# Moving one product and two pieces of one bank's traffic in a selective scan with a routed feed-forward, on one core

## The chip, the cores and the metric

The kernel runs on one core of a Trainium2 chip, in one launch. The metric is the time on the device in microseconds. TensorE is called PE, VectorE DVE, ScalarE ACT, GpSimd POOL and SyncE SP, as in the profile.

## The reference, cut to what matters

Eight sequences of 512 tokens with 256 channels go through a Mamba-like layer and then through a mixture of eight experts. Only the first layer is touched. With 512 inner channels and 16 states for each:

```
h   = silu(conv4(norm(x) @ in_proj_w.T))                  # (512 inner channels) x (512 tokens)
proj = h @ x_proj_w.T                                     # 1 + 16 + 16 rows: dt_in, B, C
dt  = softplus(dt_in @ dt_proj_w.T + dt_proj_b)
state_t = exp(A * dt_t) * state_(t-1) + B_t * h_t         # for each of 512 channels x 16 states
y_t = sum_n state_t[n] * C_t[n] + D * h_t
out = silu(y) @ out_proj_w.T + shortcut
```

All arithmetic is float32. The experts come after all eight sequences.

## The kernel before, in words

Each iteration scans one sequence `i`. Channels lie on the partitions, tokens on the free axis. A step `q` of 32 handles one state `n` (16) for one half of the channels (2), as tiles of 128 x 1024: two groups of 128 channels by 512 tokens. A step consists of:

- `decays` (ACT, L742): exp(A dt) into one of two rings in the bank `psX`, two instructions. It needs the scan two steps back.
- `inject`: the product B x into a ring of four `bx` tiles. For even `q` POOL makes it (L502), from a copy `bbc` of B's row that a DMA has spread over the partitions. For odd `q` DVE makes it (L1080), from the bank `psB`, into which PE has spread B's row with a matmul (`spread_b`, L1454) that waits for DVE's product before.
- `scan` (DVE, L1092): the recurrence along the tokens, into a ring of eight `state` tiles.
- `weigh` (POOL, L513): times C's row, in place. It waits for the scan. POOL's order in an even step is `inject(q + 4)`, then `weigh(q)`.
- `total` (PE, L1497): adds the tile up in `psY`, three steps later; the tile is then free for the scan eight steps on.

Beside this, iteration `i` carries the front of sequence `i + 1` (`front`: projection, convolution, softplus) and the back of sequence `i - 1` (`back`: output projection, norms), cut up by step numbers. Front and back share one bank, `psF`, in turn. Each engine executes its own list in the written order; semaphores connect them. What matters here:

- Step 12 and 13: ACT reads z from `psF` (L644) for the softplus. Step 14: PE multiplies the rows dt_in, B and C into `psF` (L1387, `w_bc`); ACT takes |z| (L650) and then copies the rows out into `prow` (L652).
- Steps 15 and 17: PE makes the two halves of the output projection in `psF` (L1419), the first once `prow` is copied, the second once DVE has read the first. Steps 16 and 18: DVE adds them to `ao` (L1050).
- POOL subtracts for the softplus after `weigh(20)` (`loss`, L518). ACT squares after it (L667), and DVE takes the smaller of the two in steps 23 and 24 (L1041), each after that step's scan.

Iterations 0, 1, 6 and 7 are written out; 2 to 5 run in a loop of two iterations on DVE, ACT and POOL. There the counts that semaphores are compared with are computed in registers.

Of the kernel before, what the change touches and what calls it, by code (L numbers as in the profile page):

```python
# [19 lines left out]
def build(nc, x, winT, conv_w, xprojT, dt_w, dt_b, A_log, D, woutT, norm_w, norm_b,  # L20
# [15 lines left out]
    H = 2  # L36
    CH = C // H
    Q = H * N
    PN = N // 2
    PQ = H * PN  # L40
    DQ = Q - PQ
    RD = 2
    RB = 4
    RS = 8
# [16 lines left out]
    with ctx:  # L61
# [264 lines left out]
        def _(sp):  # L326
# [30 lines left out]
            def load_b(f, par, g):  # L357
                if g == 0:
                    sp.wait_ge(rows_stored, 16 * (f + 1))
                if not (isinstance(f, int) and f == 0):  # L360
                    sp.wait_ge(pool_bx, PQ * (f - 1) + PN + CG * (g + 1))
                src = rows(f)[:, 0:N].rearrange("a (m two) t -> a two m t", two=2)[:, 0, CG * g:CG * (g + 1)]
                sp.dma_start(bbc[:, CG * g:CG * (g + 1)], src.broadcast_to([P, CG, L])).then_inc(b_loaded[g], 16)

# [119 lines left out]
        def _(pool):  # L484
# [34 lines left out]

            def iteration(i, par, do_front):  # L520
                for q in range(Q):
                    if q % 2 == 0:
                        if q + RB < Q:
                            inject(i, par, q + RB)
                        elif do_front:
                            inject(i + 1, 1 - par, q + RB - Q)
                    weigh(i, q)
                    if do_front and q == 20:
                        loss(i + 1, 1 - par)
# [57 lines left out]
        def _(act):  # L587
# [37 lines left out]
            def front(f, par, q):  # L625
# [14 lines left out]
                if q in (12, 13):  # L640
# [5 lines left out]
                    if q == 13:  # L646
                        last.then_inc(z_done, 1)
                if q == 14:
                    act.wait_ge(z_done, f + 1)
                    nc.scalar.activation(tmp[:], acc[:], ACT.Abs).then_inc(sf, 1)  # L650
                    act.wait_ge(proj_ready, f + 1)
                    nc.scalar.activation(prow[par][:], psF[:], ACT.Identity).then_inc(prow_kept, 1)  # L652
                if q == 15:
                    act.wait_ge(sf, 2 * f + 1)
                    nc.scalar.activation(tmp[:], tmp[:], ACT.Exp, scale=-1.0).then_inc(u_ready, 1)
# [329 lines left out]
        def _(dve):  # L985
# [90 lines left out]

            def inject(i, par, q):
                h, n = divmod(q, N)
                dve.wait_ge(b_bcast, i * DQ + q // 2 + 1)
                nc.vector.tensor_tensor(bx[q % RB][:], xh[par][:, h * CH:(h + 1) * CH],  # L1080
                                        psB[:].unsqueeze(1).broadcast_to([P, CH, L]), ALU.mult).then_inc(dve_bx, 1)

            def scan(i, q):
                k = i * Q + q
                if q % 2 == 0:
                    dve.wait_ge(pool_bx, i * PQ + q // 2 + 1)
                else:
                    dve.wait_ge(dve_bx, i * DQ + q // 2 + 1)
                dve.wait_ge(decay_ready, k + 1)
                if not (isinstance(k, int) and k < RS):  # L1090
                    dve.wait_ge(summed, k - RS + 1)
                nc.vector.tensor_tensor_scan(st[q % RS][:].rearrange("p c t -> p (c t)"),  # L1092
                                             decay[q % RD].rearrange("p c t -> p (c t)"),
                                             bx[q % RB][:].rearrange("p c t -> p (c t)"),
                                             0.0, ALU.mult, ALU.add).then_inc(scanned, 1)

            def iteration(i, par, do_lead, do_front, do_scan, do_back, do_choose=True):
                for q in range(Q):
                    if do_scan:
                        scan(i, q)  # L1100
                        if q % 2 == 0:
                            inject(i, par, q + 1)
                    if do_scan and not do_front and q in (12, 13, 14, 15):
                        early_act(q - 12)
                    if do_back:
                        back(i - 1, q)
                    if do_choose and q == 20:
                        choose(i - 2)
                    if do_front:
                        front(i + 1, 1 - par, q)  # L1110
                    if do_lead:
                        lead(i + 2, par, q)
# [194 lines left out]
        def _(pe):  # L1307
# [140 lines left out]
            def spread_b(i, par, q):  # L1448
# [1 line left out]
                if q == 1:  # L1450
                    pe.wait_ge(prow_kept, i + 1)
                if not (isinstance(i, int) and i == 0 and q == 1):
                    pe.wait_ge(dve_bx, i * DQ + q // 2)
                nc.tensor.matmul(psB[:], ident[:, n:n + 1].broadcast_to([P, P]), prow[par][:],  # L1454
                                 start=True, stop=True).then_inc(b_bcast, 1)

# [52 lines left out]

            def iteration(i, par, do_front, do_scan, do_back):  # L1510
                for q in range(Q):
                    if q % 2 == 1:
                        if q + 2 < Q:
                            if do_scan:
                                spread_b(i, par, q + 2)
                        elif do_front:
                            spread_b(i + 1, 1 - par, q + 2 - Q)
                    if do_scan and q >= SUM_LAG:
                        total(i, par, q - SUM_LAG)
                    elif do_back:  # L1520
                        total(i - 1, 1 - par, q + Q - SUM_LAG)
                    if do_front:
                        front(i + 1, 1 - par, q)
                    else:
                        early(q)
                    if do_back:
                        back(i - 1, q, do_front)
                    if q == 19 and i >= 2:
                        choose(i - 2)
# [170 lines left out]
```

## Time and profile before

| | us |
|---|---|
| three timed runs, median (lowest, highest) | 1506.67 (1503.97, 1511.75) |
| the profiled execution, its own time | 1497.41 |
| its span, first to last instruction | 1495.6 |
| mean granted TensorE clock, share of full | 0.904 |

The scans take up the first 1006 us of the span, the experts the rest. In the table of busy time an engine's idle time counts only where something later waits for it. The profiled execution was shorter than each of the three timed runs, so sums are made against its own time.

### The profile page before, as it was taken

Reading aid. Unit: us, or ns where it says so; the run is one execution under the profiler, and the core shown is the slowest. Engines: PE = TensorE matmul, PEld = TensorE weight load, DVE = VectorE, ACT = ScalarE, POOL = GpSimd, SP = SyncE. Lnnn points to the kernel's source line nnn. Section 1 sums busy time; section 2 is a strip of 40 time slices with the busy share of each in tenths; the row PEclk is TensorE's granted clock in tenths of the full one; section 3 lists DMA queues with packets and bytes.
Section 4 is the critical chain, followed back from the end, with each engine's and each line's share of the span. In section 5 each row is a group of like instructions: output and inputs, shape, how many; then the busy total and the mean of one; then the engine's idle time right before and its main releaser. Section 6 shows DMA issues by size and latency. Waiting matters only on the chain.

```text
span 1495.6 us, 15504 instructions
## 1 busy us (share of the span) xinstructions
PE 1187.9 (79%) x4766; PEld 523.0 (35%) x4767; DVE 1020.1 (68%) x1059; ACT 802.4 (54%) x1387; POOL 1016.0 (68%) x476
## 2 busy tenths in 40 slices
PE   4775868879878787797887877974999999999940
PEld 2221223224223222331332322423455656666620
DVE  4697998898998989899899897871311123322237
ACT  6666568658668677677766865554111111111137
POOL 0599999999999999999999999990363000000035
PEclk9897899999899899899889988996999999999975
DMA  3801301220230240240150131021954011111135
GB/s 103 320 0 58 119 23 58 98 85 31 89 123 2 99 142 2 76 164 1 58 169 1 59 127 56 1 71 56 370 202 151 0 39 42 44 47 42 39 116 179
DMA packets 78243, 129.54 MB, mean 87 GB/s; under 512 B 7648, under 2 KB 56416, under 8 KB 74080
## 3 DMA queue, kind: packets, MB, share of 16 engines
q1 hardware_dynamic: 68624, 112.07, 22.1%
q0 software_dynamic: 3072, 8.39, 1.7%
q10 hardware_dynamic: 6480, 8.26, 1.6%
q8 instruction: 32, 0.52, 0.1%
q14 instruction: 35, 0.29, 0.1%
HBM read 96.46 MB, written 32.24 MB: 86 GB/s over the span
## 4 chain that ended last, share of the span: by engine, by line
PE 35%; POOL 33%; issue 13%; DVE 11%; ACT 7%; DMA 1%; POOLq 0%; DVEq 0%; ACTq 0%
POOL state L513 19%; POOL bx L502 10%; PE psX L1606 10%; PE psX L1555 6%; DVE state L1092 5%; PE bank L1623 2%; PE psY L1623 2%; PE psY L1497 2%; POOL fy L579 2%; PE psY L1576 2%; PE bank L1576 2%; PE bank L1419 2%; DVE acc L1027 2%; POOL lt L518 1%; PE bank L1454 1%
## 5 line engine op out<-in xcount | busy, mean ns | idle before, releaser
L513 POOL TENSOR_TENSOR state<-state,cbc 128x1024 f32<-128x1024 f32 x256 | 606.2, 2390 | 11.2 <-DVE state L1092 11.0
L1092 DVE TENSOR_TENSOR_SCAN state<-psX,bx 128x1024 f32<-128x1024 f32 x256 | 577.5, 2278 | 38.0 <-ACT psX L742 23.9
L742 ACT ACTIVATE psX<-dt,aneg 128x511 f32<-128x511 f32 x512 | 330.5, 678 | 205.4 <-DVE state L1092 203.7
L502 POOL TENSOR_TENSOR bx<-xh,bbc 128x1024 f32<-128x1024 f32 x128 | 309.5, 2418 | 58.8 <-DMA bbc<-bc_rows 42.0
L1497 PE MATMUL psY<-state,ident 64*64 64x512 f32 x2048 | 293.9, 664 | 27.1 <-POOL state L513 26.8
L1454 PE MATMUL bank<-prow,ident 128*128 128x512 f32 x256 | 166.5, 737 | 114.1 <-DVE bx L1080 113.9
L579 POOL DMA_INDIRECT fy<-slot_out,slot x32 | 33.2, 1037 | 316.6 <-DMA slot_out<-yo 307.1
L1080 DVE TENSOR_TENSOR bx<-xh,bank 128x1024 f32<-128x1024 f32 x128 | 152.9, 1195 | 7.9 <-PE bank L1454 7.8
L1497 PEld LDWEIGHTS psY<-state,ident 64*64 64x64 f32 x2048 | 63.5, 142 | 218.2 <-issue 134.4
L1244 DVE TENSOR_TENSOR actN<-sg,psX 128x512 f32<-128x512 f32 x39 | 26.8, 687 | 141.3 <-ACT sg L930 141.3
L1454 PEld LDWEIGHTS bank<-prow,ident 128*128 128x128 f32 x256 | 47.3, 219 | 204.5 <-DVE bx L1080 168.0
L930 ACT ACTIVATE sg<-psX 128x512 f32<-128x512 f32 x39 | 23.3, 597 | 155.5 <-PE psX L1606 155.5
L1201 DVE TENSOR_TENSOR actS<-sg,psX 128x512 f32<-128x512 f32 x28 | 19.2, 687 | 106.5 <-ACT sg L904 106.5
L1606 PE MATMUL psX<-wg,xsT 128*128 x156 | 77.2, 617 | 1.2 <-DVE xsT L1238 0.6
L1606 PE MATMUL psX<-wu,xsT 128*128 x156 | 73.3, 592 | 0.0
L1374 PE MATMUL bank<-lt,win 128*128 128x512 f32 x112 | 55.5, 618 | 19.4 <-DVE acc L1027 18.0
L1419 PE MATMUL bank<-wout,yv 128*128 128x256 f32 x256 | 61.5, 395 | 8.9 <-ACT yv L688 7.9
L1027 DVE SCALAR_TENSOR_TENSOR acc<-bank,cw,acc 128x511 f32<-128x511 f32 (+2 forms) x84 | 62.3, 741 | 3.3 <-ACT acc L633 1.2
L904 ACT ACTIVATE sg<-psX 128x512 f32<-128x512 f32 x28 | 16.7, 597 | 81.3 <-PE psX L1555 81.3
L1419 PEld LDWEIGHTS bank<-wout,yv 128*128 128x128 f32 x256 | 48.8, 195 | 28.6 <-issue 12.7
L1555 PE MATMUL psX<-xg,shg 128*128 128x512 f32 x112 | 54.6, 611 | 1.7 <-DVE actS L1201 1.7
L1555 PE MATMUL psX<-xg,shu 128*128 128x512 f32 x112 | 52.8, 593 | 0.0
(193 smaller groups left out, 1547.3 us busy)
## 6 DMA issues: line engine op xcount, KB each, us to landing
cbc<-bc_rows SPq DMA_DIRECT2D x32, 1024.0 KB, 5.0
bbc<-bc_rows SPq DMA_DIRECT2D x16, 1024.0 KB, 6.2
slot_in<-ao SPq DMA_DIRECT2D x1, 4992.0 KB, 27.4
xsl<-slot_in SPq DMA_DIRECT2D x39, 128.0 KB, 2.2
slot_out<-yo ACTq DMA_DIRECT2D x39, 128.0 KB, 2.4
xin<-in_x SPq DMA_DIRECT2D x8, 512.0 KB, 4.4
xr<-in_x SPq DMA_DIRECT2D x8, 512.0 KB, 5.4
x_rows<-ao SPq DMA_DIRECT2D x8, 512.0 KB, 2.9
```

The source lines that it names most:

```text
L502: nc.gpsimd.tensor_tensor(bx[q % RB][:], xh[par][:, h * CH:(h + 1) * CH], bbc[:, n // 2].unsqueeze(1).broadcast_to([P, CH, L]), ALU.mult). ...
L513: nc.gpsimd.tensor_tensor(w[:], w[:], cbc[:, n].unsqueeze(1).broadcast_to([P, CH, L]), ALU.mult).then_inc(weighted, 1)
L579: nc.gpsimd.indirect_dma_start(out=fy[q % FRING][:, t % 2, :], out_offset=None, in_=y_d, in_offset=bass.IndirectOffsetOnAxis(slot[:, t:t + ...
L742: e = nc.scalar.activation(decay[q % RD][:, c, 1:L], dt[par][:, h * CH + c, 1:L], ACT.Exp, scale=aneg[:, h * CH + c, n:n + 1])
L1027: last = nc.vector.scalar_tensor_tensor(out=acc[:, c, m:L], in0=psF[:, 0:L - m], scalar=cw[:, c, TAPS - 1 - m:TAPS - m], in1=acc[:, c, m:L ...
L1080: nc.vector.tensor_tensor(bx[q % RB][:], xh[par][:, h * CH:(h + 1) * CH], psB[:].unsqueeze(1).broadcast_to([P, CH, L]), ALU.mult).then_inc ...
L1092: nc.vector.tensor_tensor_scan(st[q % RS][:].rearrange("p c t -> p (c t)"), decay[q % RD].rearrange("p c t -> p (c t)"), bx[q % RB][:].rea ...
L1419: last = nc.tensor.matmul(psF[:, (j % 2) * DIM:(j % 2 + 1) * DIM], yv[:, c, j * P:(j + 1) * P], wout[:, c], start=(c == 0), stop=(c == C - 1))
L1454: nc.tensor.matmul(psB[:], ident[:, n:n + 1].broadcast_to([P, P]), prow[par][:], start=True, stop=True).then_inc(b_bcast, 1)
L1497: done = nc.tensor.matmul(psY[o * HP:(o + 1) * HP, r], weights(half, c), src[half, c], start=first, stop=last_)
L1555: last = nc.tensor.matmul(bank, w[:, k, c * P:(c + 1) * P], xg[i][:, k], start=(k == 0), stop=(k == KC - 1))
L1606: last = nc.tensor.matmul(bank, xsT[i][:, k], w[:, bass.ds(ereg[i], 1), k].rearrange("p a n -> p (a n)"), start=(k == 0), stop=(k == KC - 1))
```

## The change

Four edits:

1. In ACT's step 14 the copy of the rows out of `psF` comes before |z|.
2. In PE's steps 15 and 17 the output projection comes before the sum (`total`) of that step, and no longer behind it.
3. The product B x of step 22 passes from POOL to DVE. DVE makes 17 of 32 products of an iteration, POOL 15.
4. All counts that go by these products follow: 15 and 17 for each iteration where 16 and 16 stood. SP's load of the next B rows (group 0) now waits for the eleventh product of POOL, that of step 20, where it waited for that of step 22.

```diff
+    BY_POOL = [q % 2 == 0 and q not in (22,) for q in range(Q)]
+    PQ = sum(BY_POOL)
     DQ = Q - PQ
+    NTH_P = [sum(BY_POOL[:q]) for q in range(Q + 1)]
+    NTH_D = [q - sum(BY_POOL[:q]) for q in range(Q + 1)]
...
-                    sp.wait_ge(pool_bx, PQ * (f - 1) + PN + CG * (g + 1))
+                    sp.wait_ge(pool_bx, PQ * (f - 1) + NTH_P[N + 2 * CG * (g + 1)])
...
-                    if q % 2 == 0:
+                    if BY_POOL[(q + RB) % Q]:
                         if q + RB < Q:
                             inject(i, par, q + RB)
...
                 if q == 14:
+                    act.wait_ge(proj_ready, f + 1)
+                    nc.scalar.activation(prow[par][:], psF[:], ACT.Identity).then_inc(prow_kept, 1)
                     act.wait_ge(z_done, f + 1)
                     nc.scalar.activation(tmp[:], acc[:], ACT.Abs).then_inc(sf, 1)
-                    act.wait_ge(proj_ready, f + 1)
-                    nc.scalar.activation(prow[par][:], psF[:], ACT.Identity).then_inc(prow_kept, 1)
...
-                dve.wait_ge(b_bcast, i * DQ + q // 2 + 1)
+                dve.wait_ge(b_bcast, i * DQ + NTH_D[q] + 1)
...
-                        if q % 2 == 0:
+                        if q + 1 < Q and not BY_POOL[q + 1]:
                             inject(i, par, q + 1)
...
-                    if q % 2 == 1:
+                    if not BY_POOL[(q + 2) % Q]:
                         if q + 2 < Q:
                             if do_scan:
                                 spread_b(i, par, q + 2)
...
+                    if do_back and q in (15, 17):
+                        back(i - 1, q, do_front)
                     if do_scan and q >= SUM_LAG:
                         total(i, par, q - SUM_LAG)
...
-                    if do_back:
+                    if do_back and q not in (15, 17):
                         back(i - 1, q, do_front)
```

PE's order around steps 14 to 18 of iteration 1 before (`xh,w_bc` is the projection of the rows, `prow,ident` the spreading of B, `wout,yv` the output projection, `state,ident` the sums, eight matmuls each, of which a row shows four where the two halves print apart):

```order
L1387 MATMUL bank<-xh,w_bc 128x512 x4
L1454 MATMUL bank<-prow,ident 128x512
L1497 MATMUL psY<-state,ident 64x512 x4
L1419 MATMUL bank<-wout,yv 128x256 x8
L1497 MATMUL psY<-state,ident 64x512 x4
L1454 MATMUL bank<-prow,ident 128x512
L1497 MATMUL psY<-state,ident 64x512 x4
L1419 MATMUL bank<-wout,yv 128x256 x8
L1497 MATMUL psY<-state,ident 64x512 x4
```

The same place now, with the line numbers of the changed file:

```order
L1390 MATMUL bank<-xh,w_bc 128x512 x4
L1457 MATMUL bank<-prow,ident 128x512
L1422 MATMUL bank<-wout,yv 128x256 x8
L1500 MATMUL psY<-state,ident 64x512 x8
L1457 MATMUL bank<-prow,ident 128x512
L1422 MATMUL bank<-wout,yv 128x256 x8
L1500 MATMUL psY<-state,ident 64x512 x8
```

One sum stood between the spreading and the first half of the projection, and none does now; the second half has also moved up by one sum.

DVE's order in steps 19 to 23 of iteration 1 before, from the scans of steps 19 and 20 on (`xh,bank` is the product B x, `psX,bx` the scan, `bank,xr` the sum for x1, `lt,dt` the minimum of step 23):

```order
L1092 SCALAR_TENSOR_TENSOR state<-psX,bx 128x1024 x2
L1080 TENSOR_TENSOR bx<-xh,bank 128x1024
L1092 SCALAR_TENSOR_TENSOR state<-psX,bx 128x1024 x2
L1080 TENSOR_TENSOR bx<-xh,bank 128x1024
L1060 TENSOR_TENSOR ao<-bank,xr 128x512
L1092 SCALAR_TENSOR_TENSOR state<-psX,bx 128x1024
L1041 SCALAR_TENSOR_TENSOR lt<-lt,dt 128x1024
```

And now:

```order
L1095 SCALAR_TENSOR_TENSOR state<-psX,bx 128x1024 x2
L1083 TENSOR_TENSOR bx<-xh,bank 128x1024
L1095 SCALAR_TENSOR_TENSOR state<-psX,bx 128x1024
L1083 TENSOR_TENSOR bx<-xh,bank 128x1024
L1095 SCALAR_TENSOR_TENSOR state<-psX,bx 128x1024
L1083 TENSOR_TENSOR bx<-xh,bank 128x1024
L1063 TENSOR_TENSOR ao<-bank,xr 128x512
L1095 SCALAR_TENSOR_TENSOR state<-psX,bx 128x1024
L1044 SCALAR_TENSOR_TENSOR lt<-lt,dt 128x1024
```

The product of step 22 now stands between the scans of steps 21 and 22, ahead of the minimum. On POOL the product of step 22 stood ahead of `weigh(18)`, and nothing took its place.

## Rows read from the trace of the kernel before

**Rows 1.** The page: the chain that ended last, by engine and by line
```profile
PE 35%; POOL 33%; issue 13%; DVE 11%; ACT 7%; DMA 1%; POOLq 0%; DVEq 0%; ACTq 0%
POOL state L513 19%; POOL bx L502 10%; PE psX L1606 10%; PE psX L1555 6%; DVE state L1092 5%; PE bank L1623 2%; PE psY L1623 2%; PE psY L1497 2%; POOL fy L579 2%; PE psY L1576 2%; PE bank L1576 2%; PE bank L1419 2%; DVE acc L1027 2%; POOL lt L518 1%; PE bank L1454 1%
```
**Rows 2.** Windows from loss to loss: stretch, length, busy us (instructions) of each engine
```profile
135.99:259.98 123.99, 91.18 (x390) 31.35 (x394) 109.32 (x80) 77.83 (x122) 116.78 (x50) 0.86 0.18 60
...
618.53:737.45 118.92, 96.82 (x416) 34.22 (x420) 108.61 (x95) 85.64 (x142) 117.51 (x51) 0.90 0.22 76
737.45:856.38 118.93, 96.00 (x432) 34.25 (x428) 107.18 (x86) 85.66 (x142) 117.61 (x51) 0.92 0.22 72
```
**Rows 3.** Waits in 618.5 to 737.4: total us, times, longest
```profile
DVE ao L1050 <- PE bank L1419: 3.6, 2, 3.1
...
POOL state L513 <- DVE state L1092: 1.4, 1, 1.4
```
**Rows 4.** Timeline of POOL, iteration 4: start, length, xcount [idle before]
```profile
611.59 2.37 POOL L513 TENSOR_TENSOR state<-state,cbc 128x1024 f32<-128x1024 f32 x1 [1.59 <-DVE state L1092]
613.92 2.35 POOL L502 TENSOR_TENSOR bx<-xh,bbc 128x1024 f32<-128x1024 f32 x1
...
618.53 4.53 POOL L518 TENSOR_TENSOR lt<-lt,dt 128x2048 f32<-128x2048 f32 x1
...
625.32 3.35 POOL L502 TENSOR_TENSOR bx<-xh,bbc 128x1024 f32<-128x1024 f32 x1
```
**Rows 5.** Timeline of DVE, iteration 4
```profile
590.00 1.19 DVE L1080 TENSOR_TENSOR bx<-xh,bank 128x1024 f32<-128x1024 f32 x1
591.38 4.47 DVE L1092 TENSOR_TENSOR_SCAN state<-psX,bx 128x1024 f32<-128x1024 f32 x2 [0.19 <-DVE bx L1080]
...
600.04 0.69 DVE L1050 TENSOR_TENSOR ao<-bank,ao 128x512 f32<-128x512 f32 x1 [3.07 <-PE bank L1419]
...
606.78 0.69 DVE L1050 TENSOR_TENSOR ao<-bank,ao 128x512 f32<-128x512 f32 x1 [0.56 <-PE bank L1419]
...
609.25 4.44 DVE L1092 TENSOR_TENSOR_SCAN state<-psX,bx 128x1024 f32<-128x1024 f32 x2
...
614.99 4.47 DVE L1092 TENSOR_TENSOR_SCAN state<-psX,bx 128x1024 f32<-128x1024 f32 x2
...
...
625.11 1.34 DVE L1041 SCALAR_TENSOR_TENSOR lt<-lt,dt 128x1024 f32<-128x1024 f32 x1 [1.75 <-ACT dt L667]
```
**Rows 6.** Timeline of PE, iteration 4
```profile
594.31 1.02 PE L1454 MATMUL bank<-prow,ident 128*128 128x512 f32 x2
595.26 1.09 PE L1497 MATMUL psY<-state,ident 64*64 64x512 f32 x8
596.28 3.72 PE L1419 MATMUL bank<-wout,yv 128*128 128x256 f32 x16
```
**Rows 7.** Timeline of ACT, iteration 4
```profile
594.51 0.60 ACT L652 ACTIVATE prow<-bank 128x512 f32<-128x512 f32 x1 [0.77 <-PE bank L1387]
...
598.03 1.28 ACT L742 ACTIVATE psX<-dt,aneg 128x511 f32<-128x511 f32 x2
...
623.09 1.91 ACT L667 ACTIVATE dt<-tmp 128x2048 f32<-128x2048 f32 x1 [2.17 <-POOL lt L518]
```
**Rows 8.** Timeline of POOL, then of DVE, iteration 0
```profile
101.23 2.35 POOL L513 TENSOR_TENSOR state<-state,cbc 128x1024 f32<-128x1024 f32 x1 [0.35 <-DVE state L1092]
...
142.50 8.25 DVE L1041 SCALAR_TENSOR_TENSOR lt<-lt,dt 128x1024 f32<-128x1024 f32 x1 [6.87 <-ACT dt L667]
```
**Rows 9.** Timeline of POOL, then of DVE, iteration 7
```profile
964.51 4.66 POOL L513 TENSOR_TENSOR state<-state,cbc 128x1024 f32<-128x1024 f32 x2
992.22 13.91 POOL L513 TENSOR_TENSOR state<-state,cbc 128x1024 f32<-128x1024 f32 x6
...
963.02 4.43 DVE L1092 TENSOR_TENSOR_SCAN state<-psX,bx 128x1024 f32<-128x1024 f32 x2
...
999.34 2.29 DVE L1092 TENSOR_TENSOR_SCAN state<-psX,bx 128x1024 f32<-128x1024 f32 x1
```

More of the change, by code:

```diff
@@ L39, in build @@
     PN = N // 2
-    PQ = H * PN
+    BY_POOL = [q % 2 == 0 and q not in (22,) for q in range(Q)]
+    PQ = sum(BY_POOL)
     DQ = Q - PQ
+    NTH_P = [sum(BY_POOL[:q]) for q in range(Q + 1)]
+    NTH_D = [q - sum(BY_POOL[:q]) for q in range(Q + 1)]
     RD = 2
@@ L1084, in scan @@
                 k = i * Q + q
-                if q % 2 == 0:
-                    dve.wait_ge(pool_bx, i * PQ + q // 2 + 1)
+                if BY_POOL[q]:
+                    dve.wait_ge(pool_bx, i * PQ + NTH_P[q] + 1)
                 else:
-                    dve.wait_ge(dve_bx, i * DQ + q // 2 + 1)
+                    dve.wait_ge(dve_bx, i * DQ + NTH_D[q] + 1)
                 dve.wait_ge(decay_ready, k + 1)
@@ L1100, in iteration @@
                         scan(i, q)
-                        if q % 2 == 0:
+                        if q + 1 < Q and not BY_POOL[q + 1]:
                             inject(i, par, q + 1)
@@ L1452, in spread_b @@
                 if not (isinstance(i, int) and i == 0 and q == 1):
-                    pe.wait_ge(dve_bx, i * DQ + q // 2)
+                    pe.wait_ge(dve_bx, i * DQ + NTH_D[q])
                 nc.tensor.matmul(psB[:], ident[:, n:n + 1].broadcast_to([P, P]), prow[par][:],
```

## The prediction, written before the changed kernel ran

> **What bounds the kernel now.** I read the chain of waits first [rows 1]. It points at POOL: its two operations of a step, L513 and L502, hold 29% of the chain, and the chain's PE part belongs mostly to the experts, which the change doesn't touch. A reader could stop here and say: every product taken from POOL is worth its duration. So the second view is one that can contradict this, the windows from one `loss` to the next [rows 2]. Such a period is 118.9 us long. POOL is busy for 117.5 us of it, DVE for 108.6 us. POOL is nearly full, but not full.
>
> The third view, the waits in the same stretch, says who holds the remaining 1.4 us: POOL waits once for a scan [rows 3]. The timelines say where. In iteration 4 `weigh(19)` starts at 611.59 after an idle 1.59 us [rows 4]; scan 19 had ended about 611.5 (the two scans 19 and 20 start at 609.25 and take 2.2 each [rows 5]). So once in each period POOL, for all its load, is released by DVE. A period is therefore a closed loop through several engines, and I follow it round:
>
> - `weigh(19)` at 611.59, product 24, `weigh(20)`, `loss` from 618.53 to 623.06 on POOL [rows 4];
> - the square on ACT, 623.09 to 625.00 [rows 7], which DVE had awaited for 1.75 us;
> - the minimum of step 23 on DVE at 625.11 [rows 5]. From there DVE works through steps 24 to 31 and 0 to 19 of the next sequence and ends scan 19 one period later.
>
> The first two legs take 625.11 - 611.59 = 13.5 us, the DVE leg 118.9 - 13.5 = 105.4 us. POOL's own loop is 118.9 - 1.4 = 117.5 us. The mixed loop is the longer, by 1.4 us, and sets the period.
>
> In the DVE leg DVE has one long wait, 3.07 us before its add at 600.04 for the first half of the output projection, and 0.56 us before the second at 606.78 [rows 5]; together 3.6 us in each period [rows 3].
>
> **Edit 1, the rows ahead of |z|.** The row that decides is the copy of the rows at 594.51: ACT had been idle for 0.77 us before it, waiting for PE [rows 7]. |z| was already over. So the copy can't come earlier by this edit: 0 us. |z|, 1.8 us, now falls behind the copy and pushes ACT's later pieces back. The first to feel it are the decays of step 18, at 598.03 now [rows 7]; with |z| ahead of them they start 1.8 us later and end at 601.1. Scan 18 follows scan 17, which starts 0.6 us after the first add, so at 599.6 with the gain of edit 2, and scan 18 at 601.8. They are 0.7 us in time. By step 19 ACT waits for DVE again, so the shift is gone. From both sides: nothing gained, since ACT waited anyway; lost at most the 1.8 us of |z| if these decays missed their scan. I take 0.
>
> **Edit 2, the projection ahead of the sums.** PE makes the spreading of B at 594.31, the sum of step 12 at 595.26 and the projection at 596.28 [rows 6]. The copy of the rows ends at 595.11 [rows 7]. With the sum behind it the projection starts at about 595.26: 596.28 - 595.26 = 1.02 us earlier. It takes as long as before, and DVE's add starts at 599.02. DVE still waits 2.05 us there. The second half starts after the first, two sums and one spreading; the distance between the halves had two sums and one spreading too, so it shifts by the same 1.02 us and isn't gained twice. Scan 19 ends 1.02 us earlier. The sums 12 and 14 come 3.7 us later, but the scans that need their tiles are those of steps 20 and 22, ten and more us away. Bounds: 0, if the first half had to wait for the copy, which leaves only 0.15 us; 3.6 us, if all of DVE's wait went. I take 1.0, since the matmuls stand without a gap between the rows.
>
> **Edit 3, the product of step 22.** POOL loses one product, 613.92 to the next start about 2.31 us later [rows 4]. It stood before `weigh(18)`, ahead of the place where POOL waits for scan 19. In a period that the mixed loop sets, this 2.31 us is only added to POOL's idle time: 1.4 + 2.3 - 1.0 = 2.7 us. It is worth 0 there.
> DVE gains the product: 1.19 us, and 0.19 us until the scan that depends on it starts, together 1.38 us (590.00 to 591.38, [rows 5]). It stands between scans 21 and 22. That is in the stretch in which DVE waits for the square: the minimum starts at 625.11 after 1.75 us of idling behind scan 23 [rows 5], which is over at 623.36. 1.75 - 1.38 = 0.37 us of cover remain, so the cost is 0. If the cover were gone, the minimum would move. PE must spread the row between product 21 and 22: product 21 is over at 614.8 and spreading takes 1.0, while DVE is at scan 21 until 617.2. Ready in time. PE waits there with sums 17 to 19 behind it, by at most 4 us; their tiles are needed at scans 25 to 27.
>
> How thin the cover is shows in the contention. DVE's minimum reads two SBUF tiles. It asks at 625.11, while POOL works; POOL's next product, at 625.32, is 3.35 us long where others are 2.35 [rows 4]: the minimum went first and POOL stood still for 1 us. In iteration 0 it went the other way: the same instruction took 8.25 us [rows 8], three POOL instructions long. The Trainium skill (SBUF — State Buffer, the section on the two separate sides) says that the pair of ports shared by the two is an exclusive lock, held for a whole instruction; by that, who comes late waits for a whole instruction of the other. The two rows agree with it in kind. It would leave the sum as it is while the minimum asks before 625.3.
>
> **Edit 4, the counts.** In the loop of iterations 2 to 5 DVE computes one more register value ahead of each product. Ahead of a product stands a scan of 2.2 us, under which the queue can work ahead: in the loop two scans in a row, with register instructions between them, take 4.44 us from start to end [rows 5], two bare durations. So 0. The upper bound is the gap that a register instruction leaves where the wait is exposed, 0.19 us [rows 5], on 13 products of the DVE leg and 4 iterations: 10 us. SP's earlier load of B rows has nobody who waits for it: 0.
>
> **The sum.** Iteration 0 has no back, and POOL runs from 101.23 on without a gap [rows 8] up to `loss`. There the product counts in full: -2.3. Iterations 1 to 6 close six mixed loops: 6 x -1.02 = -6.1. From `weigh(19)` of iteration 6 on POOL has no `loss` to share and idles no more; iteration 7's product counts, unless DVE is late. `weigh(19)` came at 964.51 + 2.31 = 966.8 and scan 19 ended at 965.2; both shift, to 964.5 and 964.3. At the end scan 31 was over at 1001.6 [rows 9], and would be at 1001.6 - 1.0 + 1.2 = 1001.8; `weigh(31)`, the last of six from 992.22, began at 1003.8 and could now begin at 1001.5. It waits 0.3: -2.0. Sum -2.3 - 6.1 - 2.0 = -10.4 us.
>
> The profiled execution took 1497.41 us, so the same execution would take 1487.0, or 0.7% less. The timed runs have their median at 1506.67, 9.3 us above the profiled one. By the same share the median is 1506.67 x 0.9931 = 1496 us, which I forecast.
>
> **Rivals.**
> A. POOL sets the period after all, because DVE's wait for the projection goes altogether (for instance ACT's and PE's work before it starts earlier too). Then each of eight iterations gives the whole product, 8 x 2.31 = 18.5 us: 1488. For it: POOL's 29% of the chain and 117.5 of 118.9 us. Against it: 2.05 us of the wait hang on the z, row and projection steps, which are not touched. 12%.
> B. Iteration 0's minimum wins against POOL this time. The loop from `loss` of iteration 0 to that of 1 would lose what it now has over the others, 124.0 - 118.9 = 5.1 us [rows 2]: 1506.67 - 15.5 = 1491. The alignment there doesn't change. 10%.
> C. The cover of 0.37 us isn't enough: the minimum asks after POOL's next instruction has begun and waits for one more, 2.3 us, in each of six periods: -10.4 + 13.9 = +3.5, 1510. It decides once scan 23 ends 0.2 us later than POOL's boundary allows, so with 0.6 us more than I reckon (ACT's later |z|, x1's sum that comes behind the product, or exposed register work). 12%.
> D. The change loses: the minimum of step 23 loses the lock to POOL, as in iteration 0, in the periods too. One such loss is 5.1 us; six are 30.6: -10.4 + 30.6 = +20, 1527. It decides from three losses on, where the gain is used up. For it: one in seven did so, and its request came at the same distance from POOL's boundary, 0.2 us, as those that won, so something that I can't see decides. Against it: six of seven won. 5%.
> E. The projection doesn't move, because the copy of the rows comes later than PE is free: only the ends gain, 4.3 us: 1502. 11%.
>
> The forecast has 50%. Less than 0.5%, 7.5 us, can't be told from no change. Faster: forecast, most of it, A and B, 66%. The same: E, C's better part, and the forecast's weak tail, 24%. Slower: D and C with exposed registers, 10%. The range leaves out D and the far end of A: 1484 to 1510; the low end is A with most of B's 5.1 us, the high end is C. The forecast's own range is 1491 to 1501.
>
> **What would show it.** The windows from loss to loss: 117.9 us, with POOL busy 115 and idle 2.7. The wait before DVE's first add: 2.05 us, where it was 3.07, and the second still 0.56. The projection's start follows the spreading without a sum between. ACT's idle before the row copy: about 2.6, where it was 0.77, and the copy no earlier. The wait for the square before the minimum: 0.4 where it was 1.75. Wrong I am if the first wait is unchanged (E), if POOL's idle stays near 1.4 at a period of 116.6 (A), if the minimum's wait is gone and the minimum lasts over 2 us (C) or over 6 us (D).

## The result, and the profile after

The changed kernel takes 1493.5 us (median of 4 runs, 1491.3 to 1493.7), the kernel before 1506.8 (4 runs beside them, 1504.0 to 1511.8). The ratio is 0.9905, with a 95% interval of 0.9877 to 0.9932: 13.3 us faster between the medians. The forecast was 1496, within 1484 to 1510. Here and below, single executions that took far longer than the rest (1526.6 us in experiment 1, 2697 in 2, 2028 in 3, 2022 in 6) are left out of the ratios and their intervals, not of the medians.

The windows from loss to loss in the trace of the changed kernel answer to [rows 2]: the stretch, its length, busy us and instructions of PE, PEld, DVE, ACT and POOL, TensorE's granted clock, the share of DMA and GB/s.

```profile
136.66:258.79 122.13, 91.97 (x402) 31.89 (x402) 115.06 (x85) 78.86 (x124) 114.43 (x49) 0.90 0.18 61
...
612.06:728.81 116.75, 96.29 (x427) 33.95 (x427) 109.74 (x95) 85.65 (x142) 115.30 (x49) 0.92 0.23 78
728.81:846.90 118.09, 94.39 (x427) 34.70 (x428) 108.43 (x87) 85.51 (x142) 115.23 (x49) 0.94 0.22 72
```

POOL has 2.2 us less to do per period, as one product of 2.35 us should give, and DVE 1.1 us more. The six periods were 124.0, 119.3, 119.2, 120.1, 118.9 and 118.9 us and are 122.1, 117.7, 116.8, 118.8, 116.8 and 118.1: 720.4 us together before, 710.3 now, so -10.1. From POOL's last wait in iteration 0, before `weigh(11)` (101.23 in [rows 8], 104.28 now), to the first loss the trace has 34.7 us before and 32.4 now, -2.3. From the last loss to the end of POOL's last operation it has 149.8 and 147.5, -2.3. The sum is -14.7 us, against -13.3 between the medians. The last operation of POOL on a state, which ended at 992.22 + 13.91 = 1006.1 [rows 9], ends at 994.5:

```profile
980.51 13.96 POOL L516 TENSOR_TENSOR state<-state,cbc 128x1024 f32<-128x1024 f32 x6
```

The two profiled executions themselves differ by less, 1497.4 and 1493.5. That is not the change. POOL's last wait in iteration 0 comes 3.05 us later than before (104.28 against 101.23), a start that varies from execution to execution: it is 100.98 in another execution of the changed kernel, the one called again below. And behind the last operation on a state the trace of before has 1495.6 - 1006.1 = 489.5 us, that of the changed kernel 497.0, and the first four experiments, in which those instructions are the same, 496.7, 497.4, 496.9 and 497.5. The profile of before caught a short execution of the experts' part, which also accounts for most of the 9.3 us that the prediction noted between it and the median.

DVE's and POOL's waits in the period from 612.1 to 728.8, and one of ACT's (total us, times, longest), answer to [rows 3]:

```profile
ACT prow L653 <- PE bank L1390: 2.6, 1, 2.6
DVE ao L1053 <- PE bank L1422: 2.2, 2, 2.0
DVE state L1095 <- ACT psX L745: 2.1, 3, 1.2
...
POOL state L516 <- DVE state L1095: 1.5, 1, 1.5
DVE lt L1044 <- ACT dt L670: 0.3, 1, 0.3
```

And here is DVE's side of iteration 4 (start, length, [idle before and who ended it]), to be held against [rows 5]:

```profile
593.94 0.69 DVE L1053 TENSOR_TENSOR ao<-bank,ao 128x512 f32<-128x512 f32 x1 [2.02 <-PE bank L1422]
...
600.33 0.69 DVE L1053 TENSOR_TENSOR ao<-bank,ao 128x512 f32<-128x512 f32 x1 [0.21 <-PE bank L1422]
...
610.74 1.20 DVE L1083 TENSOR_TENSOR bx<-xh,bank 128x1024 f32<-128x1024 f32 x1
612.12 2.29 DVE L1095 TENSOR_TENSOR_SCAN state<-psX,bx 128x1024 f32<-128x1024 f32 x1 [0.19 <-DVE bx L1083]
...
618.66 1.35 DVE L1044 SCALAR_TENSOR_TENSOR lt<-lt,dt 128x1024 f32<-128x1024 f32 x1 [0.34 <-ACT dt L670]
```

The first add waits 2.02 us where it waited 3.07, the second 0.21 where it waited 0.56. The product of step 22 stands between scans 21 and 22, and the minimum's wait fell from 1.75 us to 0.34. PE in the same iteration, against [rows 6]:

```profile
589.27 1.02 PE L1457 MATMUL bank<-prow,ident 128*128 128x512 f32 x2
590.21 3.69 PE L1422 MATMUL bank<-wout,yv 128*128 128x256 f32 x16
593.83 1.95 PE L1500 MATMUL psY<-state,ident 64*64 64x512 f32 x16
595.71 1.12 PE L1457 MATMUL bank<-prow,ident 128*128 128x512 f32 x2
596.67 3.62 PE L1422 MATMUL bank<-wout,yv 128*128 128x256 f32 x16
```

The projection follows the spreading directly, and two sums now run back to back between its halves. ACT and POOL, against [rows 7] and [rows 4]:

```profile
589.47 0.60 ACT L653 ACTIVATE prow<-bank 128x512 f32<-128x512 f32 x1 [2.60 <-PE bank L1390]
```

```profile
605.13 2.36 POOL L516 TENSOR_TENSOR state<-state,cbc 128x1024 f32<-128x1024 f32 x1 [2.93 <-DVE state L1095]
...
612.06 4.55 POOL L521 TENSOR_TENSOR lt<-lt,dt 128x2048 f32<-128x2048 f32 x1
...
618.88 3.35 POOL L505 TENSOR_TENSOR bx<-xh,bbc 128x1024 f32<-128x1024 f32 x1
```

The copy of the rows idles 2.6 us first, as forecast. POOL still waits for scan 19, here 2.93 us (1.5 to 3.0 over iterations 1 to 6). Iteration 0 still has its long minimum, as in [rows 8]. POOL, then DVE:

```profile
143.46 2.39 POOL L505 TENSOR_TENSOR bx<-xh,bbc 128x1024 f32<-128x1024 f32 x1
145.77 4.67 POOL L516 TENSOR_TENSOR state<-state,cbc 128x1024 f32<-128x1024 f32 x2
```

```profile
143.27 8.25 DVE L1044 SCALAR_TENSOR_TENSOR lt<-lt,dt 128x1024 f32<-128x1024 f32 x1 [0.72 <-ACT dt L670]
```

### The profile page after: what moved, and what is told of

Its sections match the earlier page's. It is cut to its first block, busy times and chain, and to the rows that moved or that the text cites. A ratio compares the mean times of both kernels' runs of the same rounds, so it can differ in the third digit from the quotient of the medians.

```text
span 1491.5 us, 15604 instructions
## 1 busy us (share of the span) xinstructions
PE 1188.9 (80%) x4782; PEld 525.3 (35%) x4783; DVE 1029.8 (69%) x1067; ACT 800.9 (54%) x1387; POOL 996.3 (67%) x468
## 4 chain that ended last, share of the span: by engine, by line
POOL 35%; PE 34%; issue 14%; DVE 9%; ACT 8%; DMA 1%; another core or an unknown queue 0%; ACTq 0%; POOLq 0%; DVEq 0%
POOL state L516 22%; POOL bx L505 11%; PE psX L1611 10%; PE psX L1560 6%; DVE state L1095 4%; PE bank L1628 2%; PE psY L1628 2%; POOL lt L521 2%; PE bank L1422 2%; PE bank L1581 2%; PE psY L1581 2%; PE psY L1500 1%; DVE acc L1030 1%; PE psY L1620 1%; ACT psX L745 1%
## 5 line engine op out<-in xcount | busy, mean ns | idle before, releaser
L505 POOL TENSOR_TENSOR bx<-xh,bbc 128x1024 f32<-128x1024 f32 x120 | 291.1, 2427 | 61.5 <-DMA bbc<-bc_rows 43.3
L1500 PE MATMUL psY<-state,ident 64*64 64x512 f32 x2048 | 289.0, 658 | 19.2 <-POOL state L516 19.1
L1457 PE MATMUL bank<-prow,ident 128*128 128x512 f32 x272 | 172.4, 720 | 111.6 <-DVE bx L1083 111.5
L1083 DVE TENSOR_TENSOR bx<-xh,bank 128x1024 f32<-128x1024 f32 x136 | 162.6, 1195 | 8.5 <-PE bank L1457 8.4
```

The source lines that it names most:

```text
L505: nc.gpsimd.tensor_tensor(bx[q % RB][:], xh[par][:, h * CH:(h + 1) * CH], bbc[:, n // 2].unsqueeze(1).broadcast_to([P, CH, L]), ALU.mult). ...
L1500: done = nc.tensor.matmul(psY[o * HP:(o + 1) * HP, r], weights(half, c), src[half, c], start=first, stop=last_)
```

## Experiments

Each ratio is to the kernel before, run on the same chip beside it. Experiments 8 to 11 ran on another chip than 5 to 7 and the changed kernel beside them (the kernel before took 1505.0 us there, and 1506.8), so they are compared with the changed kernel by their ratios. "Minimum" is always the first of DVE's two, the one of step 23. The first four take the change apart and set the prediction's own theory, the mixed loop through POOL, ACT and DVE (T1), against POOL's load as what sets the period (T2).

**1. Edit 1 alone**, on the kernel before:

```
 if q == 14:
+    act.wait_ge(proj_ready, f + 1)
+    nc.scalar.activation(prow[par][:], psF[:], ACT.Identity).then_inc(prow_kept, 1)
     act.wait_ge(z_done, f + 1)
     nc.scalar.activation(tmp[:], acc[:], ACT.Abs).then_inc(sf, 1)
-    act.wait_ge(proj_ready, f + 1)
-    nc.scalar.activation(prow[par][:], psF[:], ACT.Identity).then_inc(prow_kept, 1)
```

> Edit 1 alone: the rows leave the bank before |z|. Mixed-loop theory: the copy waits for PE either way, so its idle before grows from 0.77 to about 2.6 us and it starts no earlier after the projection of the rows; 0 us, ratio 1.000. Rival (the rows were late because of |z|): up to 0.8 us in each of six periods, -5 us, ratio 0.997.

Measured: 1505.9 us, ratio 0.9995 (0.9986 to 1.0005). Iteration 4's copy, on ACT:

```profile
597.95 0.60 ACT L650 ACTIVATE prow<-bank 128x512 f32<-128x512 f32 x1 [2.60 <-PE bank L1387]
```

ACT waits 1.8 us longer for PE's rows and gains nothing. Edit 1 is worth 0.

**2. Edit 2 alone**, the projection ahead of the sums:

```
+if do_back and q in (15, 17):
+    back(i - 1, q, do_front)
 if do_scan and q >= SUM_LAG:
     total(i, par, q - SUM_LAG)
...
-if do_back:
+if do_back and q not in (15, 17):
     back(i - 1, q, do_front)
```

> Edit 2 alone: the output projection ahead of the sums of steps 15 and 17. Mixed-loop theory: most of the gain inside the scans, 1.0 to 1.7 us in each of six periods, -6 to -10 us, ratio 0.993 to 0.996; DVE's waits 2.0 and 0.2 us where they were 3.07 and 0.56; POOL's idle at weigh(19) falls from 1.5 to between 0 and 0.3, and POOL becomes the bound, which cuts the gain at 1.4 to 1.5 a period. Rival (POOL's load sets the period): 0 us, ratio 1.000.

Measured: 1512.3 us, ratio 1.0028 (1.0011 to 1.0045). It is slower, where a gain was expected. The adds' waits in the period from 620.5 to 739.0 fell exactly as foreseen, but POOL's one wait is almost used up:

```profile
DVE ao L1050 <- PE bank L1419: 2.2, 2, 2.0
```

```profile
613.50 2.36 POOL L513 TENSOR_TENSOR state<-state,cbc 128x1024 f32<-128x1024 f32 x1 [0.60 <-DVE state L1092]
```

In iterations 3 and 6 POOL did not wait at all, and there the minimum took 8.25 us, with a period of 125.3 us behind iteration 3 and, behind iteration 6, a tail of 155.2 us (from the last loss to the end of POOL's last operation on a state, 149.8 before). The four periods that begin with a short minimum did shrink, by 1.1, 1.6, 0.4 and 1.4 us. POOL and DVE in iteration 3:

```profile
495.18 4.50 POOL L518 TENSOR_TENSOR lt<-lt,dt 128x2048 f32<-128x2048 f32 x1
499.65 2.34 POOL L513 TENSOR_TENSOR state<-state,cbc 128x1024 f32<-128x1024 f32 x1
501.95 2.35 POOL L502 TENSOR_TENSOR bx<-xh,bbc 128x1024 f32<-128x1024 f32 x1
504.27 4.63 POOL L513 TENSOR_TENSOR state<-state,cbc 128x1024 f32<-128x1024 f32 x2
```

```profile
501.73 8.25 DVE L1041 SCALAR_TENSOR_TENSOR lt<-lt,dt 128x1024 f32<-128x1024 f32 x1 [2.62 <-ACT dt L667]
```

While the minimum stands at 501.73, POOL does three more instructions, from 501.95 to 508.90, all of ordinary length. In [rows 4] and [rows 5] it was the other way: POOL's next one was stretched to 3.35 us and the minimum took 1.34. So edit 2 alone provokes the loss that rival D described. Two of its runs lie at 1501.5 and 1502.6 us and nine between 1510 and 1514; that would fit a number of losses that varies from execution to execution, which a time alone can't show.

**3. Edits 3 and 4 alone**: the product of step 22 on DVE with its counts (and not edits 1 and 2).

```
-    PQ = H * PN
+    BY_POOL = [q % 2 == 0 and q not in (22,) for q in range(Q)]
+    PQ = sum(BY_POOL)
```

> Edits 3 and 4 alone: DVE makes the product of step 22. Mixed-loop theory: nothing in the periods, POOL's idle per period 1.4 + 2.3 = 3.7 us; -2.3 us in iteration 0 and -2.2 us in iteration 7: -4.5 us, ratio 0.997. Rival (POOL's load sets the period): 2.3 us in each of eight iterations, -18 us, ratio 0.988.

Measured: 1503.0 us, ratio 0.9988 (0.9968 to 1.0008). The period from loss 4 to loss 5, and POOL's wait ahead of it:

```profile
617.02:736.30 119.28, 98.28 (x431) 34.90 (x428) 109.97 (x95) 85.75 (x142) 115.36 (x50) 0.90 0.22 76
```

```profile
610.07 2.36 POOL L516 TENSOR_TENSOR state<-state,cbc 128x1024 f32<-128x1024 f32 x1 [3.89 <-DVE state L1095]
```

POOL lost 2.2 us of work, its wait grew from 1.6 to 3.9 us, and the period is what it was (119.0 to 119.7 in four of the six, as 118.9 to 120.1 before; the second is 118.1, where it was 119.3). POOL's load doesn't set the period. Together experiments 2 and 3 say that the edits don't add: +0.3% and -0.1% alone, -0.9% together. The trace also answers the expected ends: iteration 0 gained its 2.3 us, but iteration 7 only 0.8 (a tail of 149.0 us), not 2.2, since POOL there waited for scans 19 and 31, 0.74 and 0.53 us.

**4. Only the projection's first half moved**: as experiment 2 with `(15,)` for `(15, 17)`.

> Of edit 2 only the first half (step 15). Mixed-loop theory: DVE's first wait falls from 3.07 to 2.05 us, its second rises from 0.56 to about 1.6 us, since the second half of the projection starts where it did; 0 us, ratio 1.000. Rival (each half is worth something by itself): -3 to -5 us, ratio 0.997 to 0.998.

Measured: 1504.5 us, ratio 0.9994 (0.9985 to 1.0002). DVE's adds:

```profile
600.98 0.69 DVE L1050 TENSOR_TENSOR ao<-bank,ao 128x512 f32<-128x512 f32 x1 [2.01 <-PE bank L1419]
608.58 0.69 DVE L1050 TENSOR_TENSOR ao<-bank,ao 128x512 f32<-128x512 f32 x1 [1.42 <-PE bank L1419]
```

The first wait falls by 1.05 us and the second rises from 0.56 to 1.42. The second half has to move too.

The losses of experiment 2 suggested a theory on the minimum, called L and later R in what follows: it loses the port to POOL when POOL has run without a wait for long, and wins when POOL has waited shortly before. The rivals are that iteration 0 is special by something else (M), or that what counts is how the two engines stand against one another in time (P).

**The changed kernel again**, beside the next three:

> The changed kernel as it stands, in the same call as three variants of it, so that these can be compared with it and not only with the kernel before. Expected 0.991 of before, seven minimums of which the first takes 8.25 us and six 1.35 us, POOL waiting 1.5 to 3.3 us at weigh(19) in iterations 1 to 6.

Measured: 1492.5 us, ratio 0.9908 (0.9894 to 0.9921). In its trace the minimum took 8.25 us in iteration 0 and 1.34 to 1.36 in the other six.

**5. One more wait on POOL in iteration 0**, on the changed kernel. It takes POOL's turn back by 1.7 us and gives nobody work:

```
-pool.wait_ge(scanned, k + 1)
+pool.wait_ge(scanned, 21 if isinstance(k, int) and k == 19 else k + 1)
```

> The changed kernel, with one wait more in iteration 0: POOL's weigh(19) also waits for scan 20, which ends about 1.7 us after POOL could start. It adds work to nobody, it only lets POOL idle once, as it idles at weigh(19) in the later iterations. Theory L (the minimum of step 23 loses POOL's lock when POOL has run without a wait from before until the minimum asks): iteration 0's minimum takes 1.35 us where it took 8.25, and the period from loss 0 to loss 1 falls from 122.1 to about 118; POOL's idling costs 1.7 us before loss 0, so in sum -2 to -3 us against the changed kernel, ratio to it 0.998. Rival M (iteration 0 is special by something else, such as the spacing of DVE's instructions): the minimum stays at 8.25 us and the kernel is 1.7 us slower, 1.001.

Measured: 1488.8 us, ratio 0.9878 (0.9863 to 0.9893), the interval clear of the changed kernel's. In iteration 0, POOL and then DVE:

```profile
132.34 2.38 POOL L516 TENSOR_TENSOR state<-state,cbc 128x1024 f32<-128x1024 f32 x1 [1.72 <-DVE state L1095]
```

```profile
145.86 1.34 DVE L1044 SCALAR_TENSOR_TENSOR lt<-lt,dt 128x1024 f32<-128x1024 f32 x1 [2.12 <-ACT dt L670]
```

The period behind it fell from 122.3 to 115.9 us. An added wait made the kernel 3.7 us faster.

**6. DVE's adds one step later**, on the changed kernel:

```
-if q in (16, 18):
+if q in (17, 19):
     h = q // 2 - 8
...
-if q == 18:
+if q == 19:
     dve.wait_ge(ao_done, 2 * b + 2)
```

> The changed kernel, with DVE's two adds of the projection moved from steps 16 and 18 to 17 and 19, where the projection's bank is long done: DVE's remaining wait of 2.0 us goes. By the mixed loop alone the period falls by 2.0 us where POOL idles as long, to 115.7, and the kernel is 10 us faster than the changed one (ratio to before 0.984). By theory L POOL's idle time at weigh(19) (1.5 us in three periods, 3 in the others) is then used up in some iterations, and there the minimum takes 8.25 us and costs 4 to 7 us: two or three such losses eat the gain, and the kernel comes out within 5 us of the changed one, with a minimum of 8.25 us in exactly those iterations in which POOL shows no wait at weigh(19). If instead all minimums stay at 1.35 us while POOL doesn't wait, theory L has fallen.

Measured: 1489.0 us (1488.4 for the three executions that the ratio rests on), ratio 0.9876 (0.9858 to 0.9895). A gain of about 4 us on the changed kernel, not of 10, but not for the reason that I had offered: POOL waited 1.0 to 2.1 us in iterations 1 to 6 (at `weigh(20)`, now), and all six minimums took 1.35. What had stood behind the add's wait came out:

```profile
592.83 2.29 DVE L1095 TENSOR_TENSOR_SCAN state<-psX,bx 128x1024 f32<-128x1024 f32 x1 [1.16 <-ACT psX L745]
595.04 0.67 DVE L1053 TENSOR_TENSOR ao<-bank,ao 128x512 f32<-128x512 f32 x1
```

The add waits for nothing, and the scan ahead of it waits 1.16 us for its decays from ACT, which the 2.0 us had covered. Since POOL waited in all six, this run doesn't test L.

**7. Product 28 on DVE too**, on the changed kernel: `q not in (22, 28)`.

> The changed kernel, with product 28 moved from POOL to DVE as well (18 on DVE, 14 on POOL). By the mixed loop DVE's leg grows by the product and the gap behind it, 1.38 us, with nothing to hide it: periods of about 119, POOL's idle time at weigh(19) 3.7 us longer, and 6 x 1.38 = 8 us slower than the changed kernel (ratio to before 0.996). If POOL set the period, each iteration would be up to 2.3 us shorter, and the kernel 14 us faster than the changed one. All six later minimums stay at 1.35 us by theory L.

Measured: 1526.1 us, ratio 1.0129 (1.0113 to 1.0144). It is slower, as the mixed loop says, but by 34 us to the changed kernel where 8 were expected. The periods are 123 us. DVE's waits from 504.5 to 627.6, three of its rows, and one of ACT's ahead of them:

```profile
DVE state L1095 <- ACT psX L745: 6.1, 5, 2.3
```

```profile
532.70 1.22 DVE L1083 TENSOR_TENSOR bx<-xh,bank 128x1024 f32<-128x1024 f32 x1 [1.03 <-PE bank L1457]
536.18 2.29 DVE L1095 TENSOR_TENSOR_SCAN state<-psX,bx 128x1024 f32<-128x1024 f32 x1 [2.26 <-ACT psX L745]
539.28 2.29 DVE L1095 TENSOR_TENSOR_SCAN state<-psX,bx 128x1024 f32<-128x1024 f32 x1 [0.81 <-ACT psX L745]
```

```profile
531.84 0.60 ACT L676 ACTIVATE dt<-bank 128x512 f32<-128x512 f32 x1 [6.38 <-PE bank L1406]
```

The product itself is 1.38 us of each period. The product behind it, of step 29, waits 1.03 us for its row, and DVE's waits for decays are 4.0 us longer than the 2.1 in the changed kernel. The trace shows where both come from. The spreading of row 28 must wait for DVE's product before, and PE stood at it for 2.94 us, until 525.30, with the front's matmuls for dt (L1404 to L1406) behind it in its list. So it was at these until 531.64 and spread row 29 only then, though DVE was done with row 28 at 529.19. And ACT waited 6.38 us for them (1.0 at most in the changed kernel), ran the decays that stand behind only at 534.87, and the scan at 536.18 waited for those. The place of a moved product matters: step 22 lies ahead of a wait that hides it, step 28 doesn't.

**8. The same length of wait, 21 us ahead of the loss**, on the changed kernel: `17 if ... k == 14`.

> The changed kernel, with one wait more in iteration 0, of the same length as in the experiment before (1.7 us) but 21 us ahead of the loss: POOL's weigh(14) also waits for scan 16. From then on POOL stands 1.7 us later against DVE, exactly as it did there, but runs the last 21 us without a wait. Theory R (what counts is that POOL waited shortly before the minimum asks): the minimum takes 8.25 us again and the kernel is 1.7 us slower than the changed one, ratio to before 0.992. Rival P (what counts is how the two engines stand against one another, and the wait only shifted that): the minimum takes 1.35 us, as there, and the ratio is 0.988.

Measured: 1492.0 us, ratio 0.9917 (0.9899 to 0.9934). In the profiled execution, POOL's wait and the minimum:

```profile
117.47 4.69 POOL L516 TENSOR_TENSOR state<-state,cbc 128x1024 f32<-128x1024 f32 x2 [1.80 <-DVE state L1095]
```

```profile
144.89 1.34 DVE L1044 SCALAR_TENSOR_TENSOR lt<-lt,dt 128x1024 f32<-128x1024 f32 x1 [2.58 <-ACT dt L670]
```

Theory R, as I had put it, expected 8.25 and missed. The six runs lie at 1487.5, 1488.2 and 1490.0, and at 1494.0, 1494.5 and 1495.2, as if half of them had a loss more; the median comes out at R's ratio of 0.992, but with the one trace against R and the runs in two groups it speaks for neither theory.

**9. A wait of half a microsecond**, on the changed kernel: `22 if ... k == 20`.

> The changed kernel, with a short wait more in iteration 0: POOL's weigh(20) also waits for scan 21, by 0.45 us, 2.3 us ahead of the loss. Theory R: even this wait is near enough, the minimum takes 1.35 us, and since POOL loses only 0.45 us the kernel is about 5 us faster than the changed one, ratio 0.987. Rival P (a shift of 1.7 us was needed): the minimum stays at 8.25 us, ratio 0.991.

Measured: 1486.7 us, ratio 0.9879 (0.9865 to 0.9894). POOL, then DVE:

```profile
134.56 2.36 POOL L516 TENSOR_TENSOR state<-state,cbc 128x1024 f32<-128x1024 f32 x1 [0.54 <-DVE state L1095]
...
143.65 3.37 POOL L505 TENSOR_TENSOR bx<-xh,bbc 128x1024 f32<-128x1024 f32 x1
```

```profile
143.47 1.35 DVE L1044 SCALAR_TENSOR_TENSOR lt<-lt,dt 128x1024 f32<-128x1024 f32 x1 [1.32 <-ACT dt L670]
```

Against P: a shift of 0.2 us of the loss (136.87 for 136.66) does what 1.7 did. In the changed kernel the minimum asked at 143.27, 0.19 us ahead of POOL's next start at 143.46, and lost. Here it asks at 143.47, 0.18 us ahead of the next start at 143.65, and wins. The distance between the two engines isn't what decides.

**10. Edit 2 alone with waits on POOL**, on the kernel of experiment 2:

```
+pool.wait_ge(scanned, k + 2 if isinstance(k, int) and k in (19, 6 * Q + 19) else k + 1)
```

> The kernel with edit 2 alone (the projection ahead of the sums), which took 1512 us with minimums of 8.25 us in iterations 0, 3 and 6; here POOL's weigh(19) also waits for scan 20 in iterations 0 and 6 (1.7 and about 1.1 us of idling), and iteration 3, inside the hardware loop, is left as it was. Theory R: the minimums of iterations 0 and 6 take 1.35 us, that of 3 may take 8.25 as before, and the kernel is 8 to 10 us faster than with edit 2 alone: about 1503, ratio 0.998. Rival (the minimum's loss depends on what DVE and PE do in these iterations and not on POOL's wait): 8.25 us in 0, 3 and 6 again and 1515 us, ratio 1.005.

Measured: 1503.6 us, ratio 0.9987 (0.9970 to 1.0004), 0.4% below experiment 2. Iteration 6, POOL and DVE, then iteration 0:

```profile
850.64 2.36 POOL L513 TENSOR_TENSOR state<-state,cbc 128x1024 f32<-128x1024 f32 x1 [0.74 <-DVE state L1092]
```

```profile
864.13 1.33 DVE L1041 SCALAR_TENSOR_TENSOR lt<-lt,dt 128x1024 f32<-128x1024 f32 x1 [4.04 <-ACT dt L667]
...
144.17 8.26 DVE L1041 SCALAR_TENSOR_TENSOR lt<-lt,dt 128x1024 f32<-128x1024 f32 x1 [6.86 <-ACT dt L667]
```

Iteration 6's minimum is short, and the tail is 149.8 us again. In iteration 0 I had misjudged: scan 20 was over before POOL came to `weigh(19)`, so the wait took no time. POOL did not idle, and the minimum was long. Iteration 3, left alone, lost as before. The time came out at my number by luck, with one loss removed and not two: in the profiled execution the tail is 5.4 us shorter and nothing else, and the runs scatter from 1494 to 1508 us.

**11. Experiments 5 and 6 together.**

> The two variants that were faster than the changed kernel put together: DVE's adds of the projection one step later (-3.6 us) and POOL's one wait in iteration 0 (-3.7 us). They act in different places, the one in iterations 1 to 7 and the other in iteration 0, so I expect the sum, 7 us less than the changed kernel: 1485, ratio 0.985. If they don't add, it is because iteration 0's gain is handed to a period in which DVE waits for ACT's decays anyway: 1488.

Measured: 1488.5 us, ratio 0.9887 (0.9872 to 0.9901): no sum of the two. Iteration 0's minimum took 1.34 us. The next one, POOL and DVE:

```profile
250.41 2.39 POOL L516 TENSOR_TENSOR state<-state,cbc 128x1024 f32<-128x1024 f32 x1
252.72 4.56 POOL L521 TENSOR_TENSOR lt<-lt,dt 128x2048 f32<-128x2048 f32 x1
257.21 2.39 POOL L516 TENSOR_TENSOR state<-state,cbc 128x1024 f32<-128x1024 f32 x1
```

```profile
259.33 8.27 DVE L1044 SCALAR_TENSOR_TENSOR lt<-lt,dt 128x1024 f32<-128x1024 f32 x1 [0.74 <-ACT dt L670]
```

With iteration 0's stall gone, POOL has no slack left in iteration 1 and runs without a wait for 122 us up to the loss; the long minimum moved there, with a period of 124.4 us. I hadn't foreseen that, though the rule that I was testing says it.

**All minimums at once.** 14 traces with seven minimums each give 98 cases. I noted for each how long before its `loss` POOL had last waited for anything. In 84 cases it was 2.3 to 20.8 us, and the minimum took 1.33 to 1.36 us. In 14 cases it was 32.4 to 124.5 us, and it took 8.25 to 8.28: iteration 0 in the ten kernels without an effective wait there, iterations 3 and 6 of experiment 2, iteration 3 of experiment 10, iteration 1 of experiment 11. No case goes the other way. The same 98 cases rule out two other causes. The minimum asked 0.16 to 0.25 us ahead of POOL's next start in the long cases and 0.17 to 0.25 in the short ones, so that distance doesn't decide (rival P); and DVE had itself idled for 0.4 to 6.9 us before it in the long cases, 0 to 4.0 in the short, which overlap as well. The limits of 20.8 and 32.4 us were read off the traces afterwards, and no run tests them. Where between 20.8 and 32.4 us it turns, and what inside the chip remembers POOL's last wait, isn't settled. That some wait shortly before is enough was tested by three added waits (experiments 5, 9 and 10); that the distance of 21 us is near the edge is only suggested by the two groups of times in experiment 8.

## Why the prediction was right, and where its numbers were off

- **The mixed loop sets the period**: shown. Taking work from POOL alone left the period at 119.3 us and lengthened POOL's wait (experiment 3); more work on DVE lengthened the period (experiment 7). Rival A's case, POOL as the bound, would have made both faster. Still, the sign that the prediction had named for A did appear. It forecast 117.9 us with POOL idle for 2.7; in the same stretch, from loss 4 to loss 5, the period is 116.75 and POOL idle for 1.45. It isn't A: DVE still waits 2.02 us for the projection's first half, and POOL is still released by scan 19. POOL's idle time is the period less its 115.3 us of work, so the sign only said that the period had fallen by more than forecast. The five periods from loss 1 on are 117.6 us in the mean (119.3 before), with POOL idle for 2.35, one by one 116.8 to 118.8 with 1.45 to 3.5.
- **Edit 1 is 0**: shown (experiment 1, ratio 0.9995), with ACT's idle of 2.60 us where 2.6 was forecast.
- **Edit 2 is -1.02 us per period**: the first wait fell by 1.05 us as worked out, and rival E is out. The step that was mis-sized is the sentence that the second half's distance stays the same and "isn't gained twice". The distance of the two adds fell from 6.74 to 6.39 us, 0.35 more. About half of that is the two sums: by the starts on PE they took 2.04 us apart (599.93 to 600.95 and 602.01 to 603.03) and take 1.88 in a row (593.83 to 595.71). The rest lies in the spreading (1.06 to 0.96) and in the second half itself (3.72 to 3.62). DVE's waits for decays fell by another 0.5 us (2.6 before, 2.1 now), which I didn't foresee. They were 2.9, 3.7 and 3.0 in the same period of experiments 1, 2 and 3, so no edit alone gives this; its cause stays open. In the period of [rows 3], 118.92 us, against 116.75 now, the account is: adds' waits -1.4, decays -0.5, the wait for the square -1.4, DVE's added work +1.1 (these two were taken to cancel, and give 0.3), together -2.2, and the period fell by 2.17. Over all six it was -10.1 instead of -6.1: the other pairs gave 0.8 to 2.4.
- **Edit 3 is 0 in the periods**: right as a sum for the whole change, and the cover came out to a few hundredths: 0.37 us forecast, 0.34 measured. Wrong as a statement on the edit. Without it edit 2 can't be had, because POOL's 1.4 us of slack are all that the loop could be shortened by; the period without losses was then 117.5 to 118.5 us, and in iterations without any slack the minimum is long (experiment 2). Edit 3 gave POOL 2.3 us of slack that keep its wait alive in iterations 1 to 6. The prediction had both figures, 1.4 and 1.02, and should have asked what happens when POOL's wait vanishes. That its total held is partly luck of the order of things: the same reasoning gave 6 to 10 us to edit 2 alone, which lost 6.
- **Iteration 0 is -2.3 and iteration 7 -2.0**: measured -2.3 and -2.3. Iteration 7's gain isn't edit 3's alone either: that edit gave 0.8 there (experiment 3) and edit 2 without a loss nothing (experiment 10, a tail of 149.8 us), the two together 2.3.
- **Edit 4 is 0**: not tried apart; with edit 3 it left the steady period where it was, so it is small.
- **Rival B** didn't happen by itself, and experiments 5 and 9 made it happen: a period shorter by 6.3 us where 5.1 were reckoned. **Rival C** did not occur: the cover held in all six, with 0.20 to 0.65 us left. **Rival D** was the right mechanism with the wrong condition. It isn't chance at equal distance, but POOL's long run without a wait. In the full change the condition is met only in iteration 0, as before, so D cost nothing new; in edit 2 alone it cost more than the whole gain.

The Trainium skill (SBUF — State Buffer, the section on the two separate sides) has whoever comes late wait for the other's instruction. The 3.35 us of POOL's product agree with that, and in kind so does the minimum's standing still. The length doesn't: 8.25 us hold three POOL instructions in a row, 143.46 to 150.4 in the changed kernel, in which the waiting DVE got no turn between any two, and the measurement decides.

The fastest versions here are those of experiments 5, 6 and 9, at ratios of 0.9878, 0.9876 and 0.9879, level within their intervals; that of 9 is the changed kernel with one wait of 0.54 us added.

## What to carry to other kernels

When an engine's only wait in a loop is about to vanish, count that as a cost and not as a success: give it slack in the same edit, and look at the instructions of the other engine that contend with it (here DVE's minimum, 1.35 or 8.25 us). Test edits alone as well as together, since here the one that "was worth nothing" was what made the other one pay. And before a wait is removed, look one row up the queue for the wait that it covers (2.0 us taken away gave 0.7 per period at most).

## What the runs showed that I had not expected

- DVE's minimum waits through three POOL instructions, 8.25 us for 1.35, in every one of the 14 cases in which POOL had run for 32 us or more without a wait, and in none of 84 in which it had waited within 21 us. It asked 2.05 us after the end of `loss` whether it won or lost, and 0.16 to 0.25 us ahead of POOL's next start in all 98. Where it went first, that next instruction of POOL took 3.32 to 3.39 us, and where it didn't, 2.35 to 2.41.
- An idle time of 0.54 us put into POOL on purpose shortened the kernel; the period behind it fell from 122.3 to 115.9 us.
- Two edits that are worth +6.3 and -3.1 us alone give -13.3 together (experiments 2 and 3, and the change; experiment 1 adds nothing), because the one supplies the slack that the other uses up.
